# Graph layer kernel: queries in twelve equal steps, constants loaded early, first keys in four PSUM banks, attention sums two blocks ahead

## What is computed

```python
xn = _layernorm(x, axis=-1)
x = x + _L0_gnn_ref(xn, edge_index, edge_type_3, ...) + _L0_mix_ref(xn[None], ...)[0]
x = x + _L0_ffn_ref(_layernorm(x, axis=-1)[None], ...)[0]
...
qf = _phi(q)          # _phi(x) = where(x > 0, x + 1, exp(x)); 12 heads of 64
kf = _phi(k)
kv = jnp.einsum('bhnd,bhne->bhde', kf, v)
y_num = jnp.einsum('bhnd,bhde->bhne', qf, kv)
y_den = jnp.einsum('bhnd,bhd->bhn', qf, z.astype(qf.dtype))   # z: kf summed over the nodes
y = (y_num / jnp.maximum(y_den[..., None], EPS))
return y @ W_out + b_out
```

## Time and profile before

| | |
|---|---|
| median of three runs | 1705.0 us (1702.95 to 1705.88) |
| the profiled execution: own time / span of the core | 1707.47 us / 1705.8 us |
| PE busy | 1566.9 us (92% of the span) |
| DVE / ACT / POOL busy | 1257.2 / 816.6 / 205.4 us |
| mean granted TensorE clock | 0.962 of 2.4 GHz |
| longest waits of PE before 465 us | 15.6 us (at 284 us), 12.5 us (at 84 us) |

### The profile page before, as it was taken

The page is one execution under the profiler, slowest core; times in us unless marked ns, Lnnn a source line. Parts: engine busy times, 40 slices in busy tenths (PEclk is TensorE's granted clock), DMA queues, the critical chain, the costliest instruction groups (busy, mean ns, idle before and its releaser), DMA issues.

```text
span 1705.8 us, 34908 instructions
## 1 busy us (share of the span) xinstructions
PE 1566.9 (92%) x10294; PEld 1112.6 (65%) x10295; DVE 1257.2 (74%) x2652; ACT 816.6 (48%) x1079; POOL 205.4 (12%) x473
## 2 busy tenths in 40 slices
PE   5699996786799999999999999989999999999987
PEld 3355564455655666689999999986555555555544
DVE  7378875775449999568899898974675477777785
ACT  6233322454124556278888888863222233343352
POOL 4011112210000000000000000000000133333340
PEclk9899997998799999999999999998999999999998
DMA  5112114440066665461004131232675531011112
GB/s 186 28 63 69 51 58 120 144 139 34 22 177 213 208 196 162 144 191 47 31 30 123 61 114 41 74 101 68 195 203 187 185 125 55 6 49 55 62 63 91
DMA packets 127716, 177.72 MB, mean 104 GB/s; under 512 B 15980, under 2 KB 99157, under 8 KB 127628
## 3 DMA queue, kind: packets, MB, share of 16 engines
q1 hardware_dynamic: 127628, 176.62, 32.9%
HBM read 119.69 MB, written 56.89 MB: 104 GB/s over the span
## 4 chain that ended last, share of the span: by engine, by line
PE 69%; issue 16%; DVE 8%; ACT 2%; DMA 2%; DVEq 1%; POOL 1%; POOLq 0%; SPq 0%; ACTq 0%
PE ps L2245 22%; PE ps L2199 14%; PE ps L2305 7%; PE ps L2304 7%; PE ps L2028 3%; PE ps L2011 2%; PE ps L2012 2%; PE ps L2013 2%; DVE oh_q L1531 1%; PE ps L2112 1%; PE ps L2316 1%; PE ps L2136 1%; DVE oh_p L1532 1%; PE ps L2182 1%; DMA tab_d<-tab 1%
## 5 line engine op out<-in xcount | busy, mean ns | idle before, releaser
L2245 PE MATMUL ps<-xrh,pf 128*128 (+1 forms) x2400 | 399.1, 329 | 4.8 <-DVE pf L1785 4.8
L2245 PEld LDWEIGHTS ps<-xrh,pf 128*128 128x128 f32 x2400 | 392.5, 190 | 11.4 <-issue 8.9
L2304 PE MATMUL ps<-x,ph 128*128 (+1 forms) x600 | 195.8, 326 | 12.5 <-POOL pl L1040 12.5
L2011 PE MATMUL ps<-w_hi,xt_hi 128*128 128x384 f16 x600 | 199.3, 332 | 3.3 <-DVE ev L1831 3.3
L1531 DVE TENSOR_SCALAR oh_q<-pat,cw 125x420 f16<-125x420 uint16 x450 | 145.0, 322 | 77.3 <-PE ps L2028 49.8
L2012 PE MATMUL ps<-w_lo,xt_hi 128*128 128x384 f16 x600 | 198.9, 332 | 0.0
L2013 PE MATMUL ps<-w_hi,xt_lo 128*128 128x384 f16 x600 | 198.6, 331 | 0.0
L1785 DVE SCALAR_TENSOR_TENSOR pf<-vb,CT 128x1260 f32<-128x1260 f32 x118 | 172.8, 1467 | 33.9 <-PE ps L2245 33.9
L2305 PE MATMUL ps<-x,ph 128*128 (+1 forms) x600 | 197.1, 329 | 0.0
L1781 DVE SCALAR_TENSOR_TENSOR vb<-vb,tb 128x1260 f32<-128x1260 f32 x118 | 170.0, 1466 | 12.8 <-ACT vb L1279 11.9
L1693 DVE CUSTOM_DVE_ANT_0 tt_junk<-kbc,mb 126x1260 bf16<-126x1260 f32 x120 | 169.1, 1466 | 12.0 <-issue 12.0
(11 more groups left out here) (279 smaller groups left out, 2416.1 us busy)
## 6 DMA issues: line engine op xcount, KB each, us to landing
qbc<-tq_d SPq DMA_DIRECT2D x12, 1260.0 KB, 6.7
wst<-in_L_gnn_W SPq DMA_DIRECT2D x60, 192.0 KB, 3.0
xr_d<-ev SPq DMA_DIRECT2D x60, 192.0 KB, 2.0
x_d<-ev SPq DMA_DIRECT2D x60, 192.0 KB, 2.4
mb_d<-mb SPq DMA_DIRECT2D x30, 310.1 KB
mb<-mb_d SPq DMA_DIRECT2D x30, 310.1 KB
xrh<-xr_d SPq DMA_DIRECT2D x3, 2880.0 KB, 15.5
x<-x_d SPq DMA_DIRECT2D x2, 3840.0 KB, 17.9
```

Source lines behind the costliest of these rows:

```text
L2011: pe.matmul(ps[:, bank, 0:CW], a_hi, hi[:, k, :], start=(k == 0 and not bias), stop=False)
L2245: mm = pe.matmul(out[b], pf[j][:, b * DB:b * DB + P], x, start=(first and b % 2 == 0), stop=False, skip_group_check=True)
L2304: pe.matmul(ps[:, bank, 0:CW], p, cols(off, off + CW), start=start, stop=False, skip_group_check=True)
```

## The change

Names as above; four things are edited.

* **Queries.** Twelve steps h (`NHQ`) replace the six blocks. A step has two of 24 query parts (`query_part(n)`: one feature block and one column group, 18 matmuls, k innermost, one bank), one window of counts and three weight tiles, used one step after they were split. `wt_hi`, `wt_lo` have six buffers each. ACT and DVE finish the two parts of a step in the next one. DVE's loop `Fori` over the blocks becomes straight code. No tile is left for the attention stage.
* **Early loads.** The loads of q1, k1, q2, k2, the biases and tiles 0 to 3 are issued after the stores of the second keys' windows (the buffers now lie where x was), and POOL splits the vectors and biases after window 17 instead of before window 33.
* **First keys.** Banks 4 to 7 and four `ev_m` buffers; block i waits for `kv_out` of block i-4; `table_sums` follows block 4.
* **Attention sums.** `weighted` uses banks 0, 1 and 6, 7 in turn and runs two blocks ahead; ACT and DVE do the small `wqk` pieces at blocks 0 and 1 instead of 2 and 3.

```diff
-        ev_m = [place(f"ev_m{j}", [P, CW], F32, 169600 + 1536 * j) for j in range(2)]
+        ev_m = [place(f"ev_m{j}", [P, CW], F32, 166400 + 1536 * j) for j in range(4)]
...
+        wt_hi = [place(f"wt_hi{j}", [P, D], F16, (75776 if j < 3 else 155376) + 1536 * j) for j in range(6)]
...
+        NHQ = 2 * K6
...
+            sp.wait_ge(ln_done, NB)
+            sp.dma_start(qkn[:, :, 0, :], q1.rearrange("(k p) h -> p k h", p=P), allow_slow_non_contiguous=True).then_inc(qk_ready, 16)
...
+            for t in range(4):
+                wq_load(t)
...
             sp.wait_ge(kvs_done, 2)
...
+            for h in range(NHQ):
+                for t in range(3 * h + 6, 3 * h + 9):
+                    wq_load(t)
+                store_window(sp, W_Q + h, cc_, h % 2)
+                if h == 3:
                     chunk_load(7)
+            sp.wait_ge(wt_lo_done, WT_TILES)
+            sp.wait_ge(ob_io, 48)
+            sp.dma_start(orow[:, :], ob_d[:, :]).then_inc(ob_io, 16)
...
-            with pool.Fori(0, W_Q) as w:
+            with pool.Fori(0, W_V + 8) as w:
                 codes_of(w)
...
-            with pool.Fori(W_Q, NWP) as w:
+            with pool.Fori(W_V + 8, NWP) as w:
...
+            for h in range(NHQ):
+                if h >= 1:
+                    exponential(2 * h - 2)
+                    exponential(2 * h - 1)
+                    late_out(W_Q + h - 1)
+                for t in range(3 * h, 3 * h + 3):
+                    wt_high(t)
+                if h == NHQ // 2:
+                    w_hi_part(C_O)
...
+            act.wait_ge(wt_used, WT_TILES)
...
+            for h in range(NHQ):
+                count_part(W_Q + h)
...
+                if h >= 1:
+                    query_out(2 * h - 2)
+                    query_out(2 * h - 1)
+                for t in range(3 * h, 3 * h + 3):
+                    wt_low(t, t % 6)
+                if h == 1:
+                    w_lo_part(5)
...
-                if i >= 2:
-                    pe.wait_ge(kv_out, i + 1)
-                product(0, xt_hi, xt_lo, i, 6 + i % 2, True).then_inc(g_done, 1)
+                if i >= 4:
+                    pe.wait_ge(kv_out, i - 1)
+                product(0, xt_hi, xt_lo, i, 4 + i % 4, True).then_inc(g_done, 1)
                 if i == 1:
                     table_rows()
-                if i == 5:
+                if i == 4:
                     table_sums()
...
+            for h in range(NHQ):
+                query_part(2 * h)
...
+                if h >= 1:
+                    wq_tile(3 * h - 3)
+                query_part(2 * h + 1)
+                count_window(W_Q + h, 6, *window(pe, W_Q + h))
+                if h >= 1:
+                    wq_tile(3 * h - 2)
+                    wq_tile(3 * h - 1)
...
-                if i >= 1:
-                    pe.wait_ge(y_n, i)
+                if i == 1:
+                    pe.wait_ge(ct_ev, NWP + 1)
+                if i >= 2:
+                    pe.wait_ge(y_n, i - 1)
...
             weighted(0)
+            weighted(1)
...
-                if i + 1 < NB:
-                    weighted(i + 1)
-                if i < 2:
-                    wq_tile(WT_TILES - 2 + i)
+                if i + 2 < NB:
+                    weighted(i + 2)
```

More of the change, by code:

```diff
@@ L168, in build @@
         rdn = [place(f"rdn{j}", [P, 2 * K6], F32, 140352 + 64 * j) for j in range(2)]
[L169 to L173, removed]
+        wt = [place(f"wt{j}", [P, D], F32, (67584, 86080, 89152, 92224, 148480, 151552)[j]) for j in range(6)]
+        wt_hi = [place(f"wt_hi{j}", [P, D], F16, (75776 if j < 3 else 155376) + 1536 * j) for j in range(6)]
+        wt_lo = [place(f"wt_lo{j}", [P, D], F16, (80384 if j < 3 else 159984) + 1536 * j) for j in range(6)]
+        qk = place("qk", [P, K6, 2, 2 * H], F16, 95552)
+        qk2 = place("qk2", [P, K6, 2, 2], F16, 95744)
         wqk_s = place("wqk_s", [P, K6, 2 * R * H], F32, 132096)
@@ L479, in build @@
         W_K, W_V, W_S, W_Q = 0, NB, 3 * NB, 3 * NB + 3
-        QW = 2
-        assert W_Q + QW * K6 == NWP and WT_TILES == K6 * K6
+        NHQ = 2 * K6
+        assert W_Q + NHQ == NWP and WT_TILES == K6 * K6
         def store_window(sp, w, stage, u):
@@ L641, in _ @@
             sp.wait_ge(kvs_done, 2)
[L642 to L660, removed]
+            for t in range(4, 6):
                 wq_load(t)
@@ L1091, in window_out, with keys @@
                 act.activation(stage[u][:, :].rearrange("p (q n) -> p q n", q=2), ps[:, bank:bank + 2, 0:QN], ACT.Copy).then_inc(ct_ev, 1)
[L1093 to L1105, removed]
+            def keys(n, bank, j):
+                act.activation(ev_m[j][:, :], ps[:, bank, 0:CW], ACT.Relu, scale=-1.0).then_inc(kv_m, 1)
+                act.wait_ge(kv_m, n + 1)
+                act.activation(ev_m[j][:, :], ev_m[j][:, :], ACT.Exp, scale=-1.0).then_inc(kv_e, 1)
+            for n in range(NB):
+                act.wait_ge(g_done, n + 1)
+                if n >= 4:
+                    act.wait_ge(kv_out, n - 1)
+                keys(n, 4 + n % 4, n % 4)
+            w_hi_part(2)
+            with act.Fori(0, NB // 2) as ii:
+                for j in range(2):
+                    n = NB + 2 * ii + j
+                    act.wait_ge(g_done, n + 1)
+                    act.wait_ge(kv_out, n + 1)
+                    keys(n, 6 + j, j)
+                    window_out(W_K + 2 * ii + j, 2 * j, cb, j, ii)
+            w_hi_part(3)
             act.wait_ge(kv_out, 2 * NB + 2)
@@ new lines, in wt_high, with exponential @@
+                if t >= 6:
+                    act.wait_ge(wt_used, t - 5)
+                act.activation(wt_hi[t % 6][:, :], wt[t % 6][:, :], ACT.Copy, scale=SPLIT).then_inc(wt_hi_done, 1)
+            def exponential(n):
+                g, q = n % NRG, n // NRG
+                act.wait_ge(q_done, n + 1)
+                if n >= NRG:
+                    act.wait_ge(q_out, n - NRG + 1)
+                act.activation(q_m[g][:, :], ps[:, g, 0:RG], ACT.Relu, bias=nbq[:, q:q + 1], scale=-1.0).then_inc(q_mm, 1)
+                act.wait_ge(q_mm, n + 1)
+                act.activation(q_m[g][:, :], q_m[g][:, :], ACT.Exp, scale=-1.0).then_inc(q_ee, 1)
@@ new lines, in _ @@
+            act.wait_ge(bq_done, 1)
+            for h in range(NHQ):
[7 more added lines that the diff above has]
+                    w_hi_part(C_O)
+            for n in range(2 * NHQ - 2, 2 * NHQ):
+                exponential(n)
+            late_out(W_Q + NHQ - 1)
@@ L1153, in _ @@
+            w_hi_part(C_O + 1)
+            act.wait_ge(wt_used, WT_TILES)
             for i in range(NB):
@@ L2074, in wq_tile @@
                 r, nb = t // K6 % R, t % K6
-                hi, lo = wt_hi[t % 3], wt_lo[t % 3]
+                hi, lo = wt_hi[t % 6], wt_lo[t % 6]
                 pe.wait_ge(wt_lo_done, t + 1)
@@ new lines, in query_part @@
+            def query_part(n):
+                g, q = n % NRG, n // NRG
+                cc, fb = C_Q + q // 3, q % 3
+                if n % (3 * NRG) == 0:
+                    pe.wait_ge(w_lo_done, cc + 1)
+                if n >= NRG:
+                    pe.wait_ge(q_out, n - NRG + 1)
+                for k in range(K6):
+                    w_h, w_l = w_hi[cc % 2][:, k, fb * P:(fb + 1) * P], w_lo[cc % 2][:, k, fb * P:(fb + 1) * P]
+                    cols = slice(g * RG, (g + 1) * RG)
+                    pe.matmul(ps[:, g, 0:RG], w_h, xt_hi[:, k, cols], start=(k == 0), stop=False)
+                    pe.matmul(ps[:, g, 0:RG], w_h, xt_lo[:, k, cols], start=False, stop=False)
+                    last = pe.matmul(ps[:, g, 0:RG], w_l, xt_hi[:, k, cols], start=False, stop=(k == K6 - 1))
+                last.then_inc(q_done, 1)
@@ new lines, in _ @@
+            for h in range(NHQ):
+                query_part(2 * h)
+                if h == 1:
+                    pe.wait_ge(kvd_done, 2)
+                    pe.wait_ge(qk_ready, 70)
+                if h >= 1:
[5 more added lines that the diff above has]
+                    wq_tile(3 * h - 1)
+            for t in range(WT_TILES - 3, WT_TILES):
+                wq_tile(t)
```

129 lines of the change are left out of this document (37 added, 92 removed).

## The result

The changed kernel takes 1626.7 us, the median of four runs (1625.51 to 1633.18); the kernel before took 1703.97 us (1702.92 to 1705.88). The ratio is 0.9553, with a 95% interval of 0.9525 to 0.9581. The profiled execution's span is 1623.5 us against 1705.8.

The account below looks back on a forecast made before the run. The prediction took PE's waits for other engines as the bound. Gains of 8.5 (first keys), 35.3 (queries) and 22 us (attention sums) made 65.8, from a median of 1705.0 to about 1639 us; range 1628 to 1656.

Parts of the forecast that it names:

- First keys, 8.5 us: First keys: with four banks block 2 needs no key sum, so `table_sums` and PE's return come 8.5 us earlier.
- Start of the queries: After the key-value sums: POOL's codes lie ready for DVE's first one-hots; part of the 35.3 us query term.
- The step of 8.46 us: Query stage: DVE sets the pace at 8.46 us for each of twelve steps; with the start, 35.3 us gained.
- the table load of 0.75 us: Query steps: DVE's table load between windows, charged in every step at 0.67 to 0.78 us.
- No load gap, 42 us: Upper bound of the query stage's gain, if DVE's load between windows costs nothing: 42 us.
- Attention sums, 22 us: Attention stage: `weighted` two blocks ahead leaves the loop; 56.8 us becomes 34.8, a gain of 22.
- the dip: Start of the attention stage: PE idle some 3 us before it, so the clock falls once; 4 us charged.
- A clock that stays low: Rival, attention stage: clock stays low and PE is the bound, gain 11 us, 1650 in all; chance 0.20.
- Steps at the old pace: Rival, query stage: a hidden round trip keeps steps at 10.1 us, gain 15.6 us, 1659 in all; chance 0.08.
- Fetches of straight code: Rival, DVE's query code: twelve stretches each run once cost up to 24 us in fetches, 1663; chance 0.05.
- The table not moving: Rival, first keys: something else holds the table's DRAM write, so its chain stays put, 1647; chance 0.07.
- Slower: Rival, query stage: the lower clock stays, PE sets steps of 14 us, 1711 in all; chance 0.03.

Follow-up runs that it names:

- the row version: Against the changed kernel: PE writes the table's 192 values as a PSUM row and DVE casts them, without the trip through DRAM; 1619.5 and 1619.6 us.

## Why the prediction was right in its places and wrong in its size

* **First keys, 8.5 us: right.** `table_sums` at 48.52 (forecast 48.5), PE back at 74.99 (75.3). Block 2 came without a gap and at full clock. The 1.0 us more by the end of the key-value sums is this 0.3 and the second keys: one slow block less, the first one longer. Alone, by the medians, the edit gave only 4.8 us (0.3 to 7.8).
* **Start of the queries: right.** No wait at 265 to 270 us; by itself it gives 10.7 us. POOL's splits at window 18 cost nothing that the trace shows.
* **The step of 8.46 us: the term that was mis-sized.** It measured 7.53 on DVE and 7.66 on PE, and the stage gave 45.6 us instead of 35.3; this is the step of the prediction that failed. The wrong piece is the table load of 0.75 us. In the earlier trace rows that gap stands, in straight code too, where DVE had just waited for ACT and one sum of 0.55 us was in front; I took it as a price of every load. As far as the runs tell, it is a price of a load behind a wait and short work, and the row at 102.38 of the same trace would have told me so. The other 0.18 us come from adding durations: successive instructions on DVE overlap by 0.1 us (296.02 + 2.70 ends at 298.72, the next begins at 298.63). With DVE at 7.53, PE's 7.66 set the step; I had 7.7 for it.
* **The upper end for the queries was worked out wrongly.** "No load gap, 42 us" should have been 35.3 + 12 x 0.75 = 44.3. The stage gave 45.6. With that end, and the others as they were, the range would have begun near 1626 and held the time, by 0.5 us. I did have the right case, as an end, and gave it no weight of its own.
* **Attention sums, 22 us: right in the mechanism, 4.9 us short.** The stage began at full clock (1.00 in its first 4 us) and its mean was 0.98. 0.9 us of it is the loop (30.8 forecast, 29.9 measured). 4 us is the dip, charged in full although it was not certain; where it comes it costs 1.5 to 2.2 us. Its premise failed with the step: I had PE idle for some 3 us just before the stage, and it was idle for 0.46. With a step of 8.39 (one more pass on DVE) PE was busy for 1.4 of the last 4 us, and the dip came.
* **The rivals.** A clock that stays low: not seen with two blocks ahead in any of nine traces, and seen at once with one block ahead, where PE waits in every block. Steps at the old pace: no; even three buffers give 8.1 us. Fetches of straight code: DVE shows no gap in steps 1 to 11, so none that counts. The table not moving: no, `table_sums` and the write behind it came 8.5 us earlier. Slower: no.
* **All errors had one sign.** Each doubtful cost (load gap, dip) was put in at its full size. So the forecast itself stood near the pessimistic end of what I knew.

## What to carry to other kernels

A gap in a trace belongs to the state in which it was seen. Before you charge it to a new order, ask whether what stood in front of it (a wait, a short instruction) is still there; a load on an engine's sequencer that is seen behind a wait can vanish in a stream that never waits. Where two engines take turns in a loop, a second block ahead removes the wait and, with it, the lower clock; count both. And look at the longest wait that an edit leaves behind: a trip through DRAM to turn a column into a row cost 17 us here, and PE and DVE did it in about one (50.87 to 51.81 us in the row version).

## What the runs showed of the hardware

* A register load from SBUF on DVE adds 0.6 to 1.0 us behind a wait and short instructions (gaps of 0.52, 1.55 and 3.40 us with one, two and five), and nothing in a stream with longer ones and no wait, at least up to five loads in a step of 7.53 us.
* The granted clock fell below full in the first 4 us of the attention stage (0.61 and 0.64, between the levels of 1.2 and 2.4 GHz) in two of seven executions without any long wait ahead of it. The first block of the first keys took 3.3 us in six traces and 4.8 to 5.9 in eight, with the same instructions (granted clock 1.00 in the changed kernel, 0.54 in the kernel with one more pass on DVE). Together that is up to 4 us of spread from run to run, and no edit's merit.
* Adding 24 us of useless matmuls to a stage in which PE waited shortened it by 4.9 us (56.7 to 51.8, one trace each), at a clock of 1.00 instead of 0.57 to 0.96.
* Two writes of 192 values of two bytes together into DRAM took 13.6 us, and reading them back 3.5.
